# Reordering the end of a block: next projections around the MLP's second product, the third norm's shift in the same period, a residual added by GpSimd

## The reference

```python
x = x + attn_block(layernorm(x))
x = x + moe(layernorm(x))

def attn_block(q_x):          # H = 16 heads of 16
    xn = ln(q_x)                          # ln1
    q, k, v = xn @ wq + bq, xn @ wk + bk, xn @ wv + bv
    fq, fk = elu(q) + 1, elu(k) + 1
    # per token: every head of q against every head of k
    kv   = einsum('bhnd,bhne->bnde', fk, v)
    qkv  = einsum('bhnd,bnde->bhne', fq, kv)
    qk   = einsum('bhnd,bnd->bhn', fq, fk.sum(heads))
    attn = qkv / (qk + 1e-6)
    x = q_x + attn @ wo + bo
    h = gelu(ln(x) @ fc_w + fc_b)         # ln2, 256 -> 1024
    return x + (h @ proj_w + proj_b)      # 1024 -> 256

def moe(x):                   # 8 experts, top 2
    out    = sum over the two chosen experts of weight * (silu(x wg) * (x wu)) w_down
    shared = (silu(x @ sg_gate.T) * (x @ sg_up.T)) @ sg_down.T
    return shared + out
```

## Time and profile before

| | |
|---|---|
| runs shown | 1877.11, 1877.44, 1881.34 us, median 1877.44 |
| the profiled execution | 1879.65 us, of which the span of the trace is 1877.6 us |
| PE busy | 1720.0 us (92%) |
| DVE busy | 1237.3 us (66%; 8 to 9 tenths in the first part) |
| POOL busy | 1244.0 us (66%; 8 to 9 tenths in the first part) |
| ACT busy | 727.7 us (39%) |
| a period of the first part | 884.1 us for twelve, 73.7 us each |

### The profile page before, as it was taken

How to read it: one execution, slowest core, us unless ns; L and a number is a source line. 1 busy time by engine, 2 the same in 40 slices (tenths; PEclk the granted TensorE clock), 3 DMA queues, 4 the chain that set the end, 5 groups by cost and what they waited for, 6 DMA issues and landing times. The chain is left out here.

```text
span 1877.6 us, 25591 instructions
## 1 busy us (share of the span) xinstructions
PE 1720.0 (92%) x7288; PEld 1242.0 (66%) x7289; DVE 1237.3 (66%) x2308; ACT 727.7 (39%) x1470; POOL 1244.0 (66%) x652
## 2 busy tenths in 40 slices
PE   2588999999999989989989999988999999999997
PEld 1354665665666656656656665657888888888886
DVE  7989899898898998998988989232222222222221
ACT  2234445445444454454454543332233232323322
POOL 5979888888898798888987987131333333333333
PEclk8788999999999999999999999988999999999999
DMA  5101100101101101001011001026777767777774
GB/s 191 45 12 45 46 26 31 57 15 43 45 23 46 45 23 46 33 23 57 14 42 45 23 35 46 18 67 187 153 164 165 154 158 166 162 153 164 165 155 86
DMA packets 87163, 148.90 MB, mean 79 GB/s; under 512 B 8640, under 2 KB 71872, under 8 KB 86720
## 3 DMA queue, kind: packets, MB, share of 16 engines
q1 hardware_dynamic: 60512, 112.58, 19.5%
q0 software_dynamic: 26592, 35.67, 11.3%
HBM read 101.79 MB, written 48.56 MB: 80 GB/s over the span
## 5 line engine op out<-in xcount | busy, mean ns | idle before, releaser
L594 POOL DMA_INDIRECT out_rows<-prod_pool,prod x142 | 220.7, 1554 | 383.9 <-ACT prod_pool L782 353.6
L487 POOL TENSOR_TENSOR prod_pool<-prod_pool 128x2048 f32<-128x2048 f32 (+2 forms) x192 | 400.6, 2087 | 15.1
L1338 PE MATMUL p_b<-bT,fc_sb 128*128 128x512 f32 x512 | 233.5, 611 | 11.9 <-ACT bT L722 11.9
L1290 PE MATMUL p_b<-proj_sb,hid 128*128 128x256 f32 x1024 | 231.6, 380 | 0.0
L1290 PEld LDWEIGHTS p_b<-proj_sb,hid 128*128 128x128 f32 x1024 | 190.1, 191 | 27.3 <-issue 0.5
L1444 PE MATMUL p_b<-prod,exp_up 128*128 128x256 f32 x840 | 187.1, 380 | 0.0
L876 DVE TENSOR_TENSOR prod<-p_q,eqk 128x4096 f32<-128x4096 f32 (+1 forms) x48 | 178.3, 3714 | 6.1 <-DVE attn L925 0.2
L1338 PEld LDWEIGHTS p_b<-bT,fc_sb 128*128 128x128 f32 x512 | 97.1, 195 | 127.2 <-issue 103.3
L885 DVE TENSOR_REDUCE p_q<-prod 128x128 f32<-128x2048 f32 x64 | 180.6, 2822 | 0.7
L899 DVE TENSOR_TENSOR prod<-p_q,v_dve 128x4096 f32<-128x4096 f32 (+1 forms) x48 | 178.2, 3713 | 2.0
L912 DVE TENSOR_REDUCE qkv<-prod 128x256 f32<-128x4096 f32 (+1 forms) x48 | 178.0, 3709 | 1.6
(11 more groups left out here) (175 smaller groups left out, 2997.0 us busy)
## 6 DMA issues: line engine op xcount, KB each, us to landing
exp_up<-in_experts SPq DMA_DIRECT2D x71, 768.0 KB, 4.5
prod<-rows_sorted SPq DMA_DIRECT2D x71, 260.0 KB, 2.8
xin<-in_x SPq DMA_DIRECT2D x16, 512.0 KB, 3.5
xres<-in_x SPq DMA_DIRECT2D x16, 512.0 KB, 4.1
out_rows<-x SPq DMA_DIRECT2D x16, 512.0 KB, 2.9
exp_dn<-in_experts SPq DMA_DIRECT2D x8, 384.0 KB, 5.6
out_rows<-prod_pool,prod POOLq DMA_INDIRECT x142, 3.8
rows_sorted<-rows SPq DMA_DIRECT2D x2, 1040.0 KB, 6.9
```

Of the source, the lines that this page charges most:

```text
L487: done(g.tensor_tensor(prod_pool[:, at:at + n * w], prod_pool[:, at:at + n * w], prod_pool[:, at + n * w:at + 2 * n * w], ALU.add))
L594: pool.indirect_dma_start(out=out[:, :], out_offset=bass.IndirectOffsetOnAxis(ap=tok_i[j][:, a:a + 1], axis=0), in_=yg[j][:, a * D:(a + 1) ...
L1290: ins = t_.matmul(o, src[:, k, t * P:(t + 1) * P], w[:, k, :], start=k == 0, stop=bias_at is None and k == chunks - 1)
L1338: ins = t_.matmul(bnk[:], fc_sb[:, k, f * P:(f + 1) * P], bT[:, k, :], start=k == 0, stop=k == KC - 1)
```

## The change

Six edits, all in the first part:

1. TensorE: P0 of the next block moves ahead of the last proj tile, P1 to right behind it, both ahead of shared_up.
2. The residual xmid is no longer multiplied into PSUM by TensorE (L1293 goes). GpSimd adds it to xres in place between its own s_pool and products, and counts xsum_ready; residual_2 and ScalarE's write of xmid wait for that.
3. ScalarE: take_qkv of u = 1 and scales_3 come ahead of the shared takes.
4. VectorE: residual_2(0) moves behind sums_1(3) and totals, residual_2(1) behind products_2(3); the statistics go straight to mv_c (L960 goes).
5. shift_3 runs at the end of the same body, first as a copy of the mean to PSUM, then one product with a PSUM and an SBUF input. pq_free at the body's end waits for it.
6. In the body that has stage_b but no core, the last block's rows are normed between the first two and the other four shared takes.

```diff
-        shift_c = tail_1[:, 16:16 + TPB]
+        shift_c = tail_0[:, 16:16 + TPB]
...                                         # Pool body, after halve(s_pool)
+                if stage_b:
+                    wait(pool, xres_loaded, 16 * c)
+                    wait(pool, ln2_var, c)
+                    announce(pool, g.tensor_tensor(xres[:], xres[:], xmid[:], ALU.add), xsum_ready, c)
...                                         # Activation body
-                    wait(act, proj_psum, 2 * (c - 1))
+                    wait(act, xsum_ready, c - 1)
                     norm(lambda t: xmid[:, t, :], lambda t: xres[:, t, :], a_scale, a_ready)
+                if stage_c and stage_b:
+                    normed_rows(c - 1, j)
                 if stage_c:
-                    normed_rows(c, j)
...
+                    wait(act, proj_psum, 2 * (c - 1))
                     norm(lambda t: hnorm[:, t, :], lambda t: xmid[:, t, :], rs_b, h_ready)
...
                     take_qkv(c + 1, 0)
-                if stage_b and not core:
+                    take_qkv(c + 1, 1)
+                if stage_b:
                     scales_3(c)
                 if stage_c:
                     table(ACT.Silu)
-                    take_shared(c)
+                    take_shared(c, range(2))
+                    if stage_b and not core:
+                        normed_rows(c, j + 1)
+                    take_shared(c, range(2, 2 * HCH))
                     table_exp_ln()
-                if more:
-                    take_qkv(c + 1, 1)
-                if stage_b and core:
-                    scales_3(c)
...                                         # Vector engine
                 if k == 1:
-                    averages(mv_b)
-                    v.tensor_copy(mv_c[:], mv_b).then_inc(x1_read, 1)
+                    averages(mv_c)
+                    dve.sem_inc(x1_read, 1)
...
-                done(v.scalar_tensor_tensor(shift_c, mv_c[:, :, 0], -1.0, rs_c[:, 0, :], ALU.mult, ALU.mult))
-                v.tensor_copy(rs_c[:, 1, :], shift_c).then_inc(ln3_scale, 1)
+                done(v.tensor_copy(shift_c, mv_c[:, :, 0]))
+                v.scalar_tensor_tensor(rs_c[:, 1, :], shift_c, -1.0, rs_c[:, 0, :], ALU.mult, ALU.mult
+                                       ).then_inc(ln3_scale, 1)
...
                     products_1(3)
+                    sums_1(3, 0, HEADS)
+                    totals(3, total[:, 0:HEADS])
                 if stage_b:
                     residual_2(c, j, 0)
                 if core:
-                    sums_1(3, 0, HEADS)
+                    wait(dve, pool_s, c + 1)
+                    done.later(v.tensor_reduce(total[:, HEADS:], s_pool[:], AX.X, ALU.add))
+                    products_2(c, 3, True)
                 if stage_b:
                     residual_2(c, j, 1)
...                                         # TensorE
-                    if plus is not None:
-                        t_.matmul(o, ident[:], plus[:, t, :], start=False, stop=False)
...
+                    def next_x(u):
+                        project_x(c + 1, u, "T")
+                        if u == 1:
+                            project_x(c + 1, 0, "P")
                     to_tokens(hid, FCH, proj_sb, (p_b0, p_b1), 4 * D, proj_psum,
                               at_last_chunk=lambda: wait(pe, gelu_ready, FCH * c),
-                              between=(lambda u: project_x(c + 1, u, "T")) if more else None,
-                              per_bank=True, plus=xmid)
+                              between=next_x if more else None, per_bank=True)
...
                 if more:
-                    project_x(c + 1, 0, "P")
+                    project_x(c + 1, 1, "P")
                 if stage_c:
                     shared_up(c)
-                if more:
-                    project_x(c + 1, 1, "P")
```

More of the change, by code:

```diff
@@ L259, in build @@
         x1_read = sem("x1_read")
+        xsum_ready = sem("xsum_ready")
         ln3_std = sem("ln3_std")
@@ L652, in take_pair, with take_shared @@
                     a.activation(dst[:, k, :], bnk[:], ACT.Copy).then_inc(ready, 1)
-            def take_shared(c):
+            def take_shared(c, parts):
                 wait(act, down_psum, c - 2)
-                for n in range(2 * HCH):
+                for n in parts:
                     wait(act, up_psum, 2 * HCH * (c - 2) + n + 1)
@@ L682, in scales_3, with normed_rows @@
                 a.activation(rs_c[:, 0, :], sq_c[:], ACT.Exp, scale=-0.5).then_inc(ln3_std, 1)
-            def normed_rows(c, j):
-                wait(act, ln3_scale, c - 1)
-                if isinstance(c, int) and c == 2:
+            def normed_rows(n, j):
+                wait(act, ln3_scale, n)
+                if isinstance(n, int) and n == 1:
                     act.wait_ge(init_stored, 48)
-                wait(act, scattered, 16 * 2 * TPB * (c - 3))
+                wait(act, scattered, 16 * 2 * TPB * (n - 2))
                 norm(lambda t: rows[j % 2][:, t, 0:D], lambda t: x1[j % 2][:, t, :], rs_c, rows_ready)
@@ L948, in residual_2 @@
                 if k == 0:
-                    wait(dve, xres_loaded, 16 * c)
+                    wait(dve, xsum_ready, c)
                     wait(dve, out_stored, 16 * (c - 2))
@@ L958, in residual_2 @@
                 if k == 1:
-                    averages(mv_b)
-                    v.tensor_copy(mv_c[:], mv_b).then_inc(x1_read, 1)
+                    averages(mv_c)
+                    dve.sem_inc(x1_read, 1)
             def shift_3(c):
-                wait(dve, ln3_std, c - 1)
-                done(v.scalar_tensor_tensor(shift_c, mv_c[:, :, 0], -1.0, rs_c[:, 0, :], ALU.mult, ALU.mult))
-                v.tensor_copy(rs_c[:, 1, :], shift_c).then_inc(ln3_scale, 1)
+                wait(dve, ln3_std, c)
+                done(v.tensor_copy(shift_c, mv_c[:, :, 0]))
+                v.scalar_tensor_tensor(rs_c[:, 1, :], shift_c, -1.0, rs_c[:, 0, :], ALU.mult, ALU.mult
+                                       ).then_inc(ln3_scale, 1)
             def choose(c, j):
@@ L1033, in body @@
                     products_1(1)
-                if stage_c:
-                    shift_3(c)
                 if core:
@@ L1104, in body @@
                 if core:
[L1105 to L1110, removed]
                     if more:
@@ L1119, in body @@
                     inverse(den_0[:, 0:2 * HEADS + POOL_HEADS])
+                if stage_b:
+                    shift_3(c)
+                if core:
                     wait(dve, pool_qkv, c + 1)
@@ L1127, in body @@
                     if more:
+                        if stage_b:
+                            dve.wait_ge(ln3_scale, c)
                         dve.sem_inc(pq_free, 1)
@@ L1280, in to_tokens @@
             def to_tokens(src, chunks, w, banks, bias_at, ready, at_last_chunk=None, between=None,
-                          per_bank=False, plus=None):
+                          per_bank=False):
                 for t in range(TPB):
```

2 lines of the change are left out of this document (added).

## The result

| | before | after |
|---|---|---|
| median (8 runs each, side by side) | 1878.12 us | 1885.18 us (1883.31 to 1888.97) |
| ratio to before | | 1.0036, 95% interval 1.0025 to 1.0047 |
| span of the profiled execution | 1877.6 us | 1881.2 us |
| a period of the steady part (mean of 11) | 73.64 us | 75.14 us |

The change makes the kernel 0.36% slower. It was forecast 0.5% faster, at 1867.5, with a range up to 1881: the median lies above the range. The lines of the changed kernel are numbered one to twelve higher: L856 is L865, L939 is L948, L954 L963, L899 L908, L1262 L1273, L1290 L1301, L1295 L1304, L1388 L1400, L965 and L966 L974 and L975, L1019 L1029.

The account below looks back on a forecast made before the run. No engine but a ring of waits bounds the kernel: 71.3 + 1.4 + 1.2 = 73.9 us a period loses 2.6 over twelve, the ends gain 12.3, so 9.7 off the profiled 1879.65; median forecast 1867.5, range 1841 to 1881.

Parts of the forecast that it names:

- The ring: From products_2's end over P1, shared products and wo (21.2), then VectorE's work back (50.1): 71.3 us a period, against 73.7.
- GpSimd's round: GpSimd's own work per period with the added residual addition: 71.8 us, a floor if the ring is longer.
- surcharges: Two additions to the ring's 71.3 us a period: 1.4 for the shared SBUF port, 1.2 for TensorE's low clock.
- The port term: VectorE's L1019 (L1029 after) waits for a GpSimd halving: 1.9 us or nearly nothing, taken as 1.4 mean per period.
- The clock term: TensorE's wait of 2.5 to 4.3 us ahead of P1 lowers its clock: 1.55 us, three periods in four, so 1.2.
- The sum: Ring plus port plus clock per period: 71.3 + 1.4 + 1.2 = 73.9 us.
- The steady part: Each period 0.2 us longer than now; twelve periods lose 2.6 us.
- The ends: Outside the steady periods 12.3 us gained: start 7.8, last full block a net loss of 5, drain 1.7, rows 5.5.
- (C): Both port and low clock cost in every period: 74.7 us a period, 1877 us, no change; chance 18%.
- (A): L1019 slips in before GpSimd's halving, leaving only the low clock's cost: 72.7 us a period, 1852 us; chance 25%.
- (B): Neither port nor low clock costs; GpSimd is the bound at 71.8 us a period: 1841 us; chance 10%.
- Rival (D): On top of (C), a second low-clock stretch falls on P2, 0.9 us a period more: 1888 us, slower; chance 12%.

Follow-up runs that it names:

- e3: Changed kernel with L1029 given only one SBUF input and two extra discarded matmuls ahead of P1: 1845.8 us, 0.9831 of before.
- e10: Changed kernel without GpSimd's residual addition (TensorE's identity product back) and with L1029 given only one SBUF input: 1851.7 us, 0.9860 of before.
- e2: Changed kernel with four extra matmuls, result discarded, filling TensorE's wait ahead of P1: 1866.9 us, 0.9940 of before.
- e1: Changed kernel with L1029 taking its reciprocal from PSUM, so only one input is in SBUF: 1850.1 us, 0.9843 of before.
- e4: Changed kernel with one more GpSimd addition of 128x128 on scratch per period: 1857.2 us, 0.9882 of before.
- e8: Changed kernel without GpSimd's residual addition, TensorE's identity product back instead: 1858.7 us, 0.9903 of before.
- e5: Kernel before, with shift_3 in its old place copying the mean to PSUM, so one SBUF input: 1842.9 us, 0.9821 of before.
- e6: Kernel before with the change's norm edits alone; projections, residual in PSUM and residual_2 stay as before: 1823.3 us, 0.9707 of before.
- e7: e6 with the router's last step also given only one SBUF input: 1823.3 us, 0.9714 of before.

## Why the prediction was wrong

Most of the mechanism stood. The steps that failed are two terms of the sum, both mis-sized: the port, put at 1.4 us a period as a mean and measured at 1.9 to 2.1 in every period, and the low clock, put at 1.2 and measured at 1.4 to 1.7 in every period. Behind both stands that they were taken as independent of each other.

- **The ring: right.** Forecast 71.3, and 71.8 for GpSimd's round. Without surcharges the period is 71.81 (e3) and, with the low clock in one period, 71.97 (e10); e3's periods in which VectorE waits at L948 are 71.7. The waits are where they were foretold: VectorE at L948 (4.2 a time, forecast some 4), TensorE ahead of P1 (4.5), POOL at the gate; none at features or residual_2. shift_3 is 0.27 in two steps (forecast 0.4).
- **The port term: mis-sized.** The prediction worked out that L1029 would come 0.3 us behind the start of a halving and pay 1.9; it came 0.28 behind (704.23) or 0.10 (779.10 against 779.00) and paid 1.9 to 2.1 above its 0.17. It then took 1.4 as a mean over periods. In the changed kernel there was no such mean: its phase was the same to 0.2 us in every period, and it paid every time. (In e2, where the periods alternate, there is one.) The worked-out value should have been the forecast.
- **The clock term: mis-sized, by a wrong independence.** It took 1.2, three periods in four; measured 1.4 to 1.7 in all (P1 at 3.40 to 3.63 against 1.96). The prediction itself noted that with the port's 1.9 TensorE's wait is 4.3, and that 4.80 had been followed by the low clock at once. The two come together, and e1 shows it from the other side: without the port the low clock comes in four periods of twelve. The runs give the cost of both as 3.33 a period (75.14 - 71.81); e1 takes 2.80 of it away and e2 1.57, which add up to more than both: taking the port away takes most of the low clock with it, while filling TensorE's wait leaves one or the other in each period.
- **The sum.** 71.3 + 2.0 + 1.55 is 74.9, against 75.14 measured. From products_2 to the wo product it is 650.53 to 673.68, 23.15, where 21.2 + 1.55 = 22.75 was worked out: the shared products take 10.85 instead of 10.47. From there to the next end of products_2 it is 52.0, forecast 50.1 + 1.9.
- **The steady part.** Forecast a loss of 0.2 a period, measured 1.5: 16.5 us over eleven. That is the miss: between the profiled executions it is 13.3 us (9.7 gained by forecast, 3.6 lost). The other four of the 17.7 between the medians are the profiled executions themselves, that of before 2.2 above its median, that of after (1883.31) 1.9 below.
- **The ends.** The start gave 9.7 us where 7.8 was forecast. Behind the last steady period 2.4 came back where -2.8 + 7.2 = 4.4 was forecast: scales_3 ahead of the shared takes adds 7.5 to the way from products_2 to residual_1 (13.5 before, 21.0 after; forecast 2.3 less 1.4), the period before gains 1.0 because L1029 slips in there, and the drain gives 8.9.
- **The rivals.** (C) happened, at 18%, with a period 0.4 longer than it had; (A) exists as e4, and (B) as e3 by its time, though not with GpSimd as the bound. Rival (D)'s second low stretch did not come in the changed kernel; a low stretch at that wait ahead of T3 came in e2, e8 and e10, where P1 kept the full clock. What ought to have put (C) first was in the text: 0.3 us inside a lock that lasts 2.36.
- **Before was misread in one place.** L965 was priced at its own 1.2 to 2.4 us. e5 shows its two lines to be worth 34 us, and e6 the norm's edits 54, with the reordering of the projections costing 28 of that again (e10 against e7). The change held one large gain, one large loss and a collision. The prediction never took the first two apart: it read one gain of 2.4 a period for the whole, ahead of the surcharges, and put the end of the wait at features(c, 1) to the credit of P1's move, which together with residual_2's makes the period 2.2 longer. Which of these moves costs most was not run apart.

By medians, step by step: before 1877, the norm's edits 1823 (e6, e7), projections, takes and residual_2 moved 1852 (e10), GpSimd's addition with the port free 1850 (e1), and L1029's input in SBUF, with the clock that follows, 1885. The steps are sizes in this order; as port and clock depend on each other, another order would divide them otherwise.

## What to carry to other kernels

Where GpSimd is busy beside VectorE, look for VectorE's small steps with two SBUF inputs on the critical ring, not only the large ones: here a step of 0.17 us cost up to 2.3, and giving it an input in PSUM cost one copy. When a period's phase is worked out and lands inside a long instruction of the other engine, forecast the full price in every period, and add what the delay does to TensorE's clock if TensorE waits behind it. When a stall is filled, look where the low clock went before calling it gone: in e2 it had only moved. And take a reordering apart before judging it: here one part of a change gained 54 us, another lost 28, and a collision lost 35.

## What was not expected of the hardware

- The Trainium skill, "SBUF — State Buffer", "SBUF: two separate sides", lets whichever of a VectorE instruction with two SBUF inputs and a GpSimd instruction starts first keep the shared port pair for its whole length, while the other is blocked. The trace agrees down to the step: 1154.17 against 1154.17 cost nothing, 0.04 us later cost 2.33; an arrival near the end of GpSimd's 4.88 us product waited for that end and got in ahead of the next instruction (e4). By this, work added to GpSimd made the kernel 28 us faster.
- A wait of 2.58 us on TensorE was followed by the low clock at 708.45 and by the full clock at 781.52, in one kernel (e1). The waits of 4.25 us and more ahead of P1 in after were followed by it every time. The wait of 1.72 ahead of T3 stands in every steady period of e2, e3, e8 and e10, and was followed by the low clock in five of eleven, none, three and one. So the length of the last wait alone does not tell; what does stays open.
- In every second of the middle periods VectorE stands 3.2 to 3.6 us ahead of features(c, 1) with no releaser in the trace. In after it stands bare; in e6 the same row alternates between a wait for ScalarE and this:

```profile
638.20 0.42 DVE L858 SCALAR_TENSOR_TENSOR eqk<-eqk,p_q 128x256 f32<-128x256 f32 x1 [2.28 <-ACT v_dve L636]
...
708.74 0.42 DVE L858 SCALAR_TENSOR_TENSOR eqk<-eqk,p_q 128x256 f32<-128x256 f32 x1 [3.41 <-issue]
```

  The middle bodies run in a loop of pairs, and it falls once per pass, so it may be the loop's turn; no run tried that. In before it was hidden under the wait for v_dve, which also alternated between 2.1 and 3.3, so P1's place can only have set the shorter of the two; that is argued from the rows, not shown by a run.
